# A fused attention and network kernel: softmax shift rows written by VectorE, another order within the rounds of the attention loop

## What is computed

```python
q = rms_norm(linear(x, q_w, q_b), norm_q_w)                # x is layer-normed before
k, k_img = rms_norm(linear(ctx_txt, ...)), rms_norm(linear(ctx_img, ...))
out = attention(q, k_img, v_img) + attention(q, k, v)      # scores / sqrt(32), softmax
x = x + linear(out, o_w, o_b)
```

## Time and profile before

| | us |
|---|---|
| median of 3 runs | 626.69 (626.53 to 627.54) |
| profiled execution, own time | 626.56 |
| its span, first to last instruction | 624.8 |
| TensorE matmuls busy | 525.3 (84%) |
| VectorE busy | 375.5 (60%) |
| ScalarE busy | 274.5 (44%) |
| GpSimd busy | 239.3 (38%) |

### The profile page before, as it was taken

How to read it: one execution, slowest core, us unless ns; L and a number is a source line. 1 busy time by engine, 2 the same in 40 slices (tenths; PEclk the granted TensorE clock), 3 DMA queues, 4 the chain that set the end, 5 groups by cost and what they waited for, 6 DMA issues and landing times.

```text
span 624.8 us, 9827 instructions
## 1 busy us (share of the span) xinstructions
PE 525.3 (84%) x3768; PEld 323.9 (52%) x3768; DVE 375.5 (60%) x782; ACT 274.5 (44%) x488; POOL 239.3 (38%) x138
## 2 busy tenths in 40 slices
PE   2689799999796898899988987898899898978961
PEld 2567678977463554545555445454444454443420
DVE  5547886136972775667666676576565745025776
ACT  3356743551151554525544343545342353545352
POOL 0033320230061674555554453426132617075353
PEclk9799999999977988999999996999999898898986
DMA  7406766797498657927997293533517124000001
GB/s 277 163 10 248 255 245 237 208 241 258 153 263 232 171 154 180 223 94 156 230 228 187 52 232 101 135 91 78 129 37 191 43 67 143 1 1 17 34 35 50
DMA packets 56327, 91.35 MB, mean 146 GB/s; under 512 B 5316, under 2 KB 30276, under 8 KB 55768
## 3 DMA queue, kind: packets, MB, share of 16 engines
q1 hardware_dynamic: 52032, 74.93, 44.1%
q0 software_dynamic: 3184, 14.16, 6.4%
q10 hardware_dynamic: 1064, 1.63, 0.8%
HBM read 70.84 MB, written 19.40 MB: 144 GB/s over the span
## 4 chain that ended last, share of the span: by engine, by line
PE 50%; DVE 21%; ACT 9%; DMA 8%; issue 7%; POOL 4%; SPq 1%; POOLq 0%; ACTq 0%; DVEq 0%
PE psum L706 11%; PE psum L780 8%; PE psum L799 8%; DMA qst<-crow 6%; PE psum L834 5%; PE psum L804 4%; DVE negt L1183 4%; PE psum L762 4%; ACT prob L1030 3%; PE psum L888 2%; PE psum L869 2%; DVE negm L1181 2%; PE psum L923 1%; POOL ssum L1353 1%; PE psum L699 1%
## 5 line engine op out<-in xcount | busy, mean ns | idle before, releaser
L1030 ACT ACTIVATE prob<-psum 128x512 f32<-128x512 f32 x256 | 141.2, 595 | 163.2 <-PE psum L780 154.5
L780 PE MATMUL psum<-qst,kst 100*128 100x256 f32 x512 | 114.3, 328 | 32.7 <-ACT prob L1030 15.6
L1183 DVE TENSOR_REDUCE negt<-psum 128x1 f32<-128x255 f32 (+1 forms) x256 | 130.6, 545 | 0.4
L780 PEld LDWEIGHTS psum<-qst,kst 100*128 100x128 f32 x512 | 79.3, 201 | 91.8 <-ACT prob L1030 45.8
L1403 POOL TENSOR_TENSOR added<-added,prob 128x1024 f32<-128x1024 f32 x48 | 114.0, 2374 | 9.4 <-ACT prob L1030 5.0
L762 PE MATMUL psum<-kst,qst 96*128 96x512 f32 x256 | 97.1, 421 | 4.3 <-DVE negt L1183 4.2
L1181 DVE TENSOR_REDUCE negm<-psum 128x1 f32<-128x257 f32 x128 | 53.4, 417 | 77.3 <-PE psum L762 76.6
L799 PE MATMUL psum<-prob,vring 128*32 128x256 f32 x1152 | 87.0, 411 | 3.6 <-DVE attT L1202 3.6
L1400 POOL TENSOR_TENSOR added<-prob 128x1024 f32<-128x1024 f32 x16 | 38.2, 2390 | 105.4 <-PE psum L804 101.6
L799 PEld LDWEIGHTS psum<-prob,vring 128*32 128x32 f32 x1152 | 35.1, 116 | 43.3 <-issue 29.0
L762 PEld LDWEIGHTS psum<-kst,qst 96*128 96x128 f32 x256 | 47.0, 200 | 9.8 <-DVE negt L1183 9.3
(11 more groups left out here) (150 smaller groups left out, 648.9 us busy)
## 6 DMA issues: line engine op xcount, KB each, us to landing
kst<-kscr SPq DMA_DIRECT2D x96, 256.0 KB, 5.5
vring<-vscr SPq DMA_DIRECT2D x16, 576.0 KB, 5.1
kscr<-hl SPq DMA_DIRECT2D x16, 512.0 KB, 3.0
d<-d POOLq DMA_DIRECT2D x8, 1024.0 KB, 6.2
qst<-qscr SPq DMA_DIRECT2D x96, 64.0 KB, 5.5
vscr<-vbuf SPq DMA_DIRECT2D x18, 256.0 KB, 3.3
raw<-ctxT SPq DMA_DIRECT2D x4, 1024.0 KB, 5.1
qscr<-hl SPq DMA_DIRECT2D x8, 512.0 KB, 3.9
```

Of the source, the lines that this page charges most:

```text
L780: mm = pe.matmul(score2[:, j * QH:(j + 1) * QH], kst[0:100, slot, jj, k0:k0 + P], qst[0:100, slot, jj, :], start=True, stop=True)
L1030: act.activation(prob[:, r % NP, part], score2[:, part], ACT.Exp).then_inc(exp2_done, 1)
L1183: dve.tensor_reduce(negt[:, u % 2, qt, half, j:j + 1], psum[:, n % 3, k0:512], AX.X, ALU.max, negate=True)\
```

## The change

Three parts. First, the shift rows: `maxes` writes 16 columns per query tile (image and text for four heads, twice), `shift` is a plain product with the identity into partitions 96 to 111 of bank 7, and VectorE writes the four heads' rows of `qst` itself with one scalar_tensor_tensor of 16 partitions by 1024 elements: value plus `lows` (0 or -1) times its rounded copy. There is no DMA and no step of SP. The indicator table has a block of 16 rows for each head (ind_in: 64 by 1024 instead of 4 by 1024), and `lows` is one more constant to load.

Second, the end of a unit: ScalarE first copies the value bank to `pvc`, which lets the next unit's values begin; Ln and Exp then work in place in the bank of sums, and `attn_done` is awaited only before the next sums (chunk 5).

Third, the order of a round: S2(r,0), S2(r,1), S1(t,0), S1(t,1), S1(t+1,0), S2(r+1,0), S2(r+1,1), S1(t+1,1), extras of r, shift, PV, PV, extras of r+1. maxes comes between the first two S2. The copy stands before S2(r,0) and Ln and Exp after the scores of round r % 8 == 2; weigh is in the round r % 8 == 4, before S2(r+1,1). The projections move from 4 to 6 (`o`), the small network starts at step 73 instead of 71, and the last step becomes 150. The lines after S1 of steps 10 and 11 are the same steps written otherwise.

```diff
-    shifts = range(4, 8 * NU, 8)
+    shifts = range(5, 8 * NU, 8)
-    s = 8 * 8 + 7
+    s = 8 * 8 + 9
     at(s, 'ch_row')
...
-        s = 8 * NG * (k + 1) + (4 if k < 3 else 2)
+        s = 8 * NG * (k + 1) + (6 if k < 3 else 2)
...
+        if evict:
+            add('attn', u, 0)
+        if scores:
+            add('S2', r, 0)
+            if r % 8 == 0 and r > 0 and r // 8 + 2 < NU:
+                add('load', r // 8 + 2)
         if t % 8 == 0 and t // 8 <= NU:
             add('maxes', t // 8 - 1)
         if scores:
             add('S2', r, 1)
         if keys:
             add('S1', t, 0)
             add('S1', t, 1)
+            add('S1', t + 1, 0)
         if scores:
             add('S2', r + 1, 0)
+        if r % 8 == 4 and 0 <= u < NU - 1:
+            add('weigh', u)
         if scores:
             add('S2', r + 1, 1)
         if keys:
             add('S1', t + 1, 1)
+        if evict:
+            add('attn', u, 1)
+            add('attn', u, 2)
         side(r)
         extras(r)
+        if t % 8 == 0 and t // 8 <= NU:
+            add('shift', t // 8 - 1)
...
-                    pe.wait_ge(shift_loaded[u % 2], 16 * 2 * (u // 2 + 1))
+                    pe.wait_ge(shift_written, u + 1)
...
-                    mm = pe.matmul(score2[:, j * QH:(j + 1) * QH], kst[0:100, slot, jj, k0:k0 + P],
-                                   qst[0:100, slot, jj, :], start=True, stop=True)
+                    mm = pe.matmul(score2[:, j * QH:(j + 1) * QH], kst[0:96 + 4 * HPG, slot, jj, k0:k0 + P],
+                                   qst[0:96 + 4 * HPG, slot, jj, :], start=True, stop=True)
...
-                        pe.wait_ge(sum_emptied, u)
-                        pe.wait_ge(attn_done, u)
+                        pe.wait_ge(pv_emptied, u)
...
                 if c == N_ADDED:
+                    if u > 0:
+                        pe.wait_ge(attn_done, u)
...
-                    mm = pe.transpose(ps[0:8, qt * P:(qt + 1) * P], negm[:, u % 2, qt * 8:qt * 8 + 8], ident[:, :])
+                    mm = pe.matmul(ps[96:96 + 4 * HPG, qt * P:(qt + 1) * P], negm[:, u % 2, qt], ident[:, :], start=True, stop=True)
...
-                    act.activation(r, psum[:, SUM_BANK, :], ACT.Ln).then_inc(sum_emptied, 1)
+                    act.copy(pvc[:].rearrange("p s n -> p (s n)"), psum[:, PV_BANK, :]).then_inc(pv_emptied, 1)
                 elif part == 1:
-                    act.wait_ge(sum_emptied, u + 1)
-                    act.activation(r, r, ACT.Exp, scale=-1.0).then_inc(rsum_done, 1)
+                    act.activation(sums, sums, ACT.Ln).then_inc(sum_logged, 1)
+                else:
+                    act.wait_ge(sum_logged, u + 1)
+                    act.activation(sums, sums, ACT.Exp, scale=-1.0).then_inc(rsum_done, 1)
...
-                if u >= 1:
-                    dve.wait_ge(shift_loaded[(u - 1) % 2], 16 * 2 * ((u + 1) // 2))
+                slot = pair_slot(u, 0)[0]
                 dve.wait_ge(job_done, job + 1)
-                src = psum[0:8, bank_of[job], 0:QH]
-                link(dve.tensor_copy(crow[:, 0, :], src))
-                dve.tensor_tensor(crow[:, 1, :], src, crow[:, 0, :], ALU.subtract).then_inc(emptied_by['dve'], 1)
+                rows_of = slice(96, 96 + 4 * HPG)
+                src = psum[rows_of, bank_of[job], 0:QH]
+                link(dve.tensor_copy(crow[rows_of, :], src))
+                ins = dve.scalar_tensor_tensor(qst[rows_of, slot:slot + 2].rearrange("p a b n -> p (a b) n"),
+                                               crow[rows_of, :].rearrange("p (o n) -> p o n", o=1).to_broadcast([4 * HPG, 4, QH]), lows[rows_of, 0:1],
+                                               src.rearrange("p (o n) -> p o n", o=1).to_broadcast([4 * HPG, 4, QH]), ALU.mult, ALU.add)
+                ins.then_inc(emptied_by['dve'], 1)
+                dve.wait_ge(emptied_by['dve'], emptied(job)[1])
+                dve.engine_nop().then_inc(shift_written, 1)
```

More of the change, by code:

```diff
@@ L240, in make_plan @@
             s += 1 if k < 3 else 0
-    for t in range(10, ahead):
-        s1(t)
+    s1(10)
+    s1(ahead - 1)
     last = max(max(extra), 8 * NU + 2)
@@ L293, in make_plan @@
             if r == 8 * NU:
-                for part in range(2):
+                for part in range(3):
                     add('attn', NU - 1, part)
@@ L401, in build @@
         xterms = sb("xterms", [P, 2, 8], F32, o); o += 64
-        crow = sb("crow", [8, 2, QH], F32R, o); o += 2 * KB_
+        crow = sb("crow", [P, QH], F32R, o); o += KB_
+        lows = sb("lows", [P, 1], F32, o); o += 32
         assert o % 32 == 0
@@ L482, in build @@
         negm_done = sem("negm_done")
-        shift_loaded = [sem(f"shift_loaded{i}") for i in range(2)]
+        shift_written = sem("shift_written")
         s2_done = sem("s2_done")
@@ L650, in load_v @@
                 sp.dma_start(vring[:, u % 2], vscr[b, :, :, P * g:P * (g + 1)].rearrange("c p n -> p c n")).then_inc(v_loaded[u % 2], 16)
[L652 to L658, removed]
             def ch_row():
@@ L670, in f_out @@
                   .then_inc(out_stored, 16)
-            steps = {'split': split, 'norm': norm, 'vstore': vstore, 'load': load, 'load_v': load_v, 'phase2': phase2, 'shift': shift,
+            steps = {'split': split, 'norm': norm, 'vstore': vstore, 'load': load, 'load_v': load_v, 'phase2': phase2,
                      'ch_row': ch_row, 'f_out': f_out}
@@ L937, in _ @@
         def _(act):
-            for dst, src in ((ident[:, :], T['ident']), (colp[:], T['cols']), (ind_in[:, :], T['ind'])):
+            for dst, src in ((ident[:, :], T['ident']), (colp[:], T['cols']), (ind_in[:, :], T['ind']), (lows[:, :], T['lows'])):
                 act.dma_start(dst, src).then_inc(const_loaded, 16)
@@ L1032, in attn @@
             def attn(u, part):
-                r = rsum[:].rearrange("p s n -> p (s n)")
+                sums = psum[:, SUM_BANK, :]
                 if part == 0:
@@ L1460 @@
     eye = np.eye(P, dtype=np.float32)
-    ind = np.zeros((4, KEYS), np.float32)
-    ind[0::2, :IMG] = 1
-    ind[1::2, IMG:] = 1
+    ind = np.zeros((HPG, 2, 2, HPG, KEYS), np.float32)
+    for j in range(HPG):
+        ind[j, :, 0, j, :IMG] = 1
+        ind[j, :, 1, j, IMG:] = 1
+    ind = ind.reshape(4 * 4 * HPG, KEYS)
+    lows = np.zeros((P, 1), np.float32)
+    lows[96 + 2 * HPG:96 + 4 * HPG] = -1
     host = {
@@ L1474 @@
         'd1_b': get('L0_ffn_d1_b'),
-        'ident': eye, 'ind': ind, 'sel': np.tile(eye[:32, :32], (4, 1)),
+        'ident': eye, 'ind': ind, 'lows': lows, 'sel': np.tile(eye[:32, :32], (4, 1)),
     }
```

49 lines of the change are left out of this document (19 added, 30 removed).

## The result

The changed kernel takes 637.22 us (median of 4 runs, 634.48 to 639.11), the kernel before beside it 626.61 (623.21 to 627.54). The ratio is 1.018, 95% interval 1.012 to 1.023: slower by 1.8%, where 621.2 and at most 632 were forecast. Any kernel here has a slower execution now and then; times and ratios are of the others. The profiled execution after took 634.48 us with a span of 632.6, the fastest of its four; so the traces are 7.8 us apart and the medians 10.6.

The account below looks back on a forecast made before the run. Rounds were taken as bound by different things, with 13.1 us of TensorE waits for one transfer. -13.1 + 0.85 - 4 + 5.3 + 5.5 - 1.5 + 1.5 = -5.45, so 621.2 us against the 626.69 median; range 610 to 632.

Parts of the forecast that it names:

- the transfer: The qst<-crow transfer S2 waited for, 13.1 us in 7 waits; forecast to go wholly, -13.1 us.
- start: Before the main units: larger constants cost 0.5 us, and the first unit's new write ahead of S2 costs 0.85.
- loads +1: Key loads of unit 3 needed some 6 us sooner: +1 us, bounds 0 and 5.9.
- units 9 to 15: Units with the small network between: shared-bank jobs wait for the longer shift; sum +5.5 us, bounds -2 and +14.
- c2: Unit's second round, named by its first chunk; value products wait for the copy alone, -0.95 us, to 3.3 to 3.5.
- c4: Unit's third round, from chunk 4; holds weigh and the longer shift, grows from 3.43 to about 4.05 us.
- c6: Unit's fourth round, from chunk 6; fourth score matmul waits for VectorE 1 to 1.4 us, round +1.2, near 5.9.
- Clock: Three clock falls after transfer waits cost 5.7 us; gain taken as -4, bounds 0 and -5.7.
- gate matmuls now fill that: -2.15: Tail: TensorE's 2.15 us wait for Ln, Exp and weigh after the last value products is filled; tail sum -1.5.
- (b): Rival: VectorE's queue decides the unit, slower; 632 us at a 2.0 us operation; chance 0.20, shared with the half rate.
- half rate: Skill's rule for two wide SBUF sources, left out of the sum; operation about 2.3 us, total 637; within (b)'s 0.20.
- (d): Rival: it cancels, clock falls stay since c6 idles 1.2 us in each unit; 625 to 626 us, chance 0.07.

Follow-up runs that it names:

- Experiment 1: Changed kernel with one step moved: in c6 the fourth score matmul stands behind the value products; 613.8 us, ratio 0.976.
- experiment 7: Changed kernel with its wide operation cut from 1024 to 256 elements from unit 3 on; 616.97 us, ratio 0.978.
- experiment 5: Kernel of Experiment 1 with the small network and last tiles starting at step 71 instead of 73; 621.19 us, ratio 0.984.
- experiment 4: Kernel of Experiment 1 with the shift step moved behind the extras of the fifth chunk; 611.06 us, ratio 0.967.
- experiments 2: Kernel before with only the shift rows written by VectorE, in the old order; 622.2 us, ratio 0.989.
- experiments 10: Kernel before with only the value bank copy, reciprocals in place and later weigh; transfers and round order as before; 626.95 us, ratio 1.000.
- experiment 12: Kernel of experiment 4 with ind_in and lows loaded only after half of x has come; 611.14 us, ratio 0.973.
- experiment 9: Kernel before with the new constants alone and 16 instead of 4 indicator rows placed per head; 632.38 us (one run).
- experiment 3: Changed kernel's shift rows and reciprocals, with weigh in c4, in the old round order and old step numbers; 640.6 us, ratio 1.019.

## Why the prediction was wrong

By the stages of the sum, against the profiled execution (span, us). Of the 13.1 us for the transfer, 1.6 belong to the start: the wait ahead of the first S2.

| | forecast | measured |
|---|---|---|
| start (0.5, 0.85 at the first unit, -1.6) | -0.2 | +1.4 |
| units 0 to 8 (-11.5, -4, +5.3, loads +1) | -9.2 | -6.2 |
| units 9 to 15 | +5.5 | +9.1 |
| tail | -1.5 | +3.5 |
| sum | -5.45 | +7.8 |

*Right.* The transfer's 13.1 us went, and no S2 waits for one. With them went 1.64 us that the forecast had not counted, a wait ahead of the S2 at 216.47 in unit 2 that the timeline puts down to issue; like the others it is absent where VectorE writes the rows. The operation was forecast at 1.27 us and took 1.29. c2 at 3.43 (3.3 to 3.5), c4 at 3.83 (near 4.05). In c6 the fourth score product waits for VectorE and not for anything else, 1.39 us (1 to 1.4). Without a fall c6 took 6.38 where 5.9 was forecast: the wait is 0.2 longer and TensorE's own work 4.98 instead of 4.7. A clean unit takes 18.4 us without a fall (17.9 forecast) and 20.0 with one. No S1 waits for keys, so the microsecond for loads was not there.

*The step that failed* is *Clock*, and the sentence "New waits of about 1.2 us come (below), between these." It asked only whether the three old falls would stay (0 to -5.7, taken as -4). It didn't ask for new ones, though the change puts a wait of nearly the smallest of them (1.42) into every unit. Two waits of the kernel before that it did not weigh, 1.18 and 1.63 us (ahead of 256.79 and 337.51), had no fall, so a fall behind 1.4 us was no certainty, but it was a price to set. The old falls did go, but five new ones came. Each c6 with one took 7.7 to 8.1 us against 6.38 and one pushed its end into the next c0: 8.1 us together. Without them the time would be some 629 us (an estimate from the median less 8.1), still above the forecast but inside the range. Experiment 1 (the wait gone, falls gone, -19.7 us in these units) and experiment 7 (the wait cut to 0.59, falls gone, -13.1) show it by taking the cause away in two ways.

*Tail: the sign was wrong.* "gate matmuls now fill that: -2.15" had them fill the wait ahead of the last projection. They do stand there, but ahead of it in order, so it waits for them. The timeline of the tail:

```profile
574.39 0.61 PE L797 MATMUL psum<-prob,ones 128*32 128x256 f32 x8
574.93 3.70 PE L918 MATMUL psum<-wg,xTt 128*128 128x512 f32 x8
578.72 7.11 PE L829 MATMUL psum<-wbuf,attT 128*128 128x512 f32 x16
...
607.30 6.62 PE L918 MATMUL psum<-wg,xTt 128*128 128x512 f32 x8 [0.77 <-ACT xTt L1064]
```

The projection begins 3.7 us after the last value products, where it began 2.7 us after them before. And at 607.30 a gate product takes 6.62 us instead of 3.67, at a low clock. The kernel before has a fall there too, but a shorter one:

```profile
600.76 5.33 PE L923 MATMUL psum<-wg,xTt 128*128 128x512 f32 x8 [0.77 <-ACT xTt L1067]
```

Between the two traces the +3.5 us split so: the projection begins 1.0 us later and takes 1.7 less (7.11 for the 8.77 of the earlier trace rows), this gate product takes 1.3 more, and the gaps between the tiles behind the projection are 2.9 us longer. In experiment 7 the same steps take 56.06 with 5.30 for this product, so some 1.7 of the 3.5 us goes with the longer fall. The rest goes with the sixth gate tile: kernels with five tiles behind the loop have tails of 54.1 to 55.1 us. Why the tiles then stand further apart no experiment shows; experiment 5 doesn't separate it either.

*Units 9 to 15.* The mechanism forecast (jobs of the fifth chunk wait for the wide operation) is there: 2.8, 2.4, 1.3 and 1.0 us, 7.5 in all where 8.5 was forecast. But the stretches split the loss into 5.6 us more idle time (24.3 to 30.0) and 3.5 us more busy time, and the forecast had no term for the second. Nor does it end when the waits go (experiment 4). Shift rows alone lose 6.1 us there and the reciprocals alone 3.9 (experiments 2 and 10), so both parts have a share. What decides beyond that is open: the interplay of the network's steps, ScalarE's exponentials and the clock was moved by every experiment and explained by none.

*Start.* The two costs sum to nearly what was measured, but by luck: with the transfer's wait of 1.6 us gone from the start, the forecast is -0.2. The first unit's write takes less than that wait gave (in experiment 12 the first S2 comes 1.3 us sooner than before). The constants were sized at 0.5 and cost 2.4 in experiment 9, 1.6 of it by a fall of the clock at 77 us.

*The rivals.* (b) ended on the right side, but its condition, an operation of 1.64 us or more, did not come true. The half rate of the Trainium skill ("Vector Engine (DVE) Microarchitecture Reference", section 7) is not seen: 490 ns for 256 elements and 1290 for 1024 are 1.04 ns an element. One of its two sources is in PSUM; the L1166 row, with both in SBUF, doesn't show it either. What happened is nearest to (d), falls that stay because c6 idles in each unit, with 0.07; its price took as many falls as before, where there were more, and left out tail and units 9 to 15. The range ended at 632, the price of a slower operation; with (d) priced at one fall in each of six clean units, 1.6 us each on top of its 625 to 626, it would have reached 635, still short of 637.2: the rest is the tail and units 9 to 15.

## What to carry to other kernels

When a change makes an engine late inside a loop that is otherwise busy, price the wait twice: once by its length and once by what the clock does after it, and count how often it comes, for 1.4 us of waiting cost another 1.6 in five units of eight. In a queue served in order, put the instruction that waits behind those that don't need what it waits for; here that one line was worth some 4%. Two parts that are each harmless can share one slack, so sum what an engine has to do between two fixed points over all parts before any of them is called hidden.

## What was not expected of the hardware

Waits of 0.42 and 0.59 us in every clean unit were followed by no fall of the clock, of 1.39 us by one in five of eight, always beginning in the round of the wait, of 1.42 us in experiment 3 by one in three of six, and of 1.58 us once by none (unit 1 of experiment 7, round of 6.6 us). In the kernel before 1.42 and 1.64 us had one, 1.18 and 1.63 none; in its second profile 1.14 us had one and 1.46 none. So the length of a wait alone doesn't decide. Less idle time did not always mean a higher clock: experiment 4 has 5.5 us less of it than experiment 1 in units 9 to 15 and a clock of 0.90 instead of 0.93. And the new constants (256 KB, and the small `lows`) loaded in the first microseconds brought a fall at 77 us, reproducibly: all ten traces with the new constants loaded at once have it, and the four others (the kernel before twice, experiments 10 and 12) don't.
